# Attention scores as 32-row products of one head each, in place of block-diagonal products over all 128 rows

## What is computed

```python
x = x + xattn(layernorm(x), ctx, ctx, mask, Wq, Wk, Wv, Wo)
x = x + ffn(layernorm(x), wg, w1, w3, w2)
# xattn: 16 heads, head_dim 8
scores = einsum('bhqd,bhkd->bhqk', Q, K) / sqrt(8)
scores = where(mask == 0, -1e9, scores)
out    = einsum('bhqk,bhkd->bhqd', softmax(scores), V) ... @ Wo.T
# ffn: top 2 of 8 experts by x @ wg.T, each silu(x @ w1.T) * (x @ w3.T) @ w2.T
```

## Time and profile before

| | us |
|---|---|
| median of three executions | 288.39 |
| lowest and highest | 286.16, 289.48 |
| span of the profiled execution (first to last instruction) | 289.2 |
| TensorE busy, share of the span | 220.1 (76%) |
| VectorE busy | 214.5 (74%) |
| ScalarE busy | 131.9 (46%) |
| GpSimd busy | 109.8 (38%) |
| mean granted clock of TensorE | 0.877 of full speed |

### The profile page before, as it was taken

The page is one execution under the profiler, slowest core; times in us unless marked ns, Lnnn a source line. Parts: engine busy times, 40 slices in busy tenths (PEclk is TensorE's granted clock), DMA queues, the critical chain, the costliest instruction groups (busy, mean ns, idle before and its releaser), DMA issues.

```text
span 289.2 us, 5289 instructions
## 1 busy us (share of the span) xinstructions
PE 220.1 (76%) x1445; PEld 161.4 (56%) x1445; DVE 214.5 (74%) x619; ACT 131.9 (46%) x291; POOL 109.8 (38%) x120
## 2 busy tenths in 40 slices
PE   0787779998989988887667674688787789997620
PEld 0663456666757665665336542477566668886410
DVE  4779966688759867895977786568895568775596
ACT  5777127554665448342145546243334435453300
POOL 4310350121403070105486556104556565555530
PEclk9996579999999999979756799589899999999855
DMA  6954411353033302331602110421342232211807
GB/s 216 318 233 118 131 35 28 92 125 86 9 98 96 94 0 67 87 100 47 207 9 67 46 39 29 99 47 30 77 79 76 82 84 73 80 52 26 236 5 217
DMA packets 38108, 26.33 MB, mean 91 GB/s; under 512 B 4748, under 2 KB 35726, under 8 KB 37696
## 3 DMA queue, kind: packets, MB, share of 16 engines
q1 hardware_dynamic: 34848, 19.76, 25.5%
q0 software_dynamic: 2656, 5.40, 6.1%
q10 hardware_dynamic: 576, 0.83, 0.9%
HBM read 12.32 MB, written 6.31 MB: 64 GB/s over the span
## 4 chain that ended last, share of the span: by engine, by line
PE 42%; DVE 30%; issue 10%; SPq 8%; DMA 4%; ACT 2%; POOL 1%; another core or an unknown queue 1%; DVEq 0%; ACTq 0%; POOLq 0%
SPq L427 8%; PE bank L528 8%; DVE m_neg L1411 6%; PE bank L759 4%; PE bank L760 3%; PE bank L733 3%; PE bank L652 3%; DMA bd<-st 3%; PE bank L746 3%; PE bank L736 3%; PE bank L693 2%; PE bank L676 2%; PE bank L734 2%; PE bank L679 2%; PE bank L534 2%
## 5 line engine op out<-in xcount | busy, mean ns | idle before, releaser
L1411 DVE TENSOR_REDUCE m_neg<-bank 128x4 f32<-128x512 f32 x64 | 43.5, 684 | 15.4 <-PE bank L693 15.0
L1048 POOL DMA_INDIRECT ys<-big x39 | 38.1, 976 | 40.0 <-DVE big L1447 19.2
L923 ACT ACTIVATE big<-bank 128x512 f32<-128x512 f32 x64 | 37.4, 597 | 20.9 <-PE bank L679 20.0
L797 ACT ACTIVATE st<-bank 128x128 fp32r<-128x128 f32 (+1 forms) x78 | 22.6, 330 | 31.6 <-PE bank L746 16.1
L1004 POOL DMA_INDIRECT xg<-rows,rows_i x24 | 24.6, 1027 | 31.8 <-DVE rows_i L1218 11.6
L693 PE MATMUL bank<-bd,st 128*128 128x512 f32 x64 | 31.1, 509 | 4.7 <-DMA bd<-st 3.8
L676 PE MATMUL bank<-m_bd,ones_b 128*128 128x512 f32 x64 | 31.3, 489 | 2.1 <-ACT big L923 1.9
L759 PE MATMUL bank<-bd,st 128*128 x78 | 24.3, 332 | 9.8 <-DVE big L1447 6.2
L1355 DVE SCALAR_TENSOR_TENSOR st<-st_hi,cst,bank 128x512 fp32r<-128x512 f32 x32 | 23.3, 747 | 11.3 <-ACT st_hi L797 9.0
L1026 POOL TENSOR_TENSOR m_bd<-mT,cst 128x512 fp32r<-128x512 f32 x16 | 17.3, 1110 | 30.1 <-DVE mT L1334 30.0
L679 PE MATMUL bank<-bd,st 128*128 128x512 f32 x64 | 27.1, 423 | 0.0
(11 more groups left out here) (174 smaller groups left out, 514.0 us busy)
## 6 DMA issues: line engine op xcount, KB each, us to landing
bd<-st SPq DMA_DIRECT2D x126, 64.0 KB, 2.0
big<-xg SPq DMA_DIRECT2D x39, 64.5 KB
raw<-in_L_ffn_w SPq DMA_DIRECT2D x2, 1024.0 KB, 9.3
raw<-ys SPq DMA_DIRECT2D x6, 256.0 KB
x_all<-in_x SPq DMA_DIRECT2D x4, 256.0 KB, 4.5
rows<-in_mask_BxS_if POOLq DMA_DIRECT2D x4, 256.0 KB, 5.2
ctx_all<-in_L_ffn_w SPq DMA_DIRECT2D x1, 1024.0 KB
ctx_all<-in_ctx SPq DMA_DIRECT2D x3, 256.0 KB, 5.2
```

The costliest lines, as they stand in the source:

```text
L923: nc.scalar.activation(prob[n % 2][:, NJ * g:NJ * (g + 1), :].rearrange("p h q -> p (h q)"), s2[k % 2][:, :], ACT.Exp, scale=SCALE).then_i ...
L1048: pool.indirect_dma_start(ys, bass.IndirectOffsetOnAxis(xt[n % XR][:, D:RW].bitcast(I32), 0), y_sb[n % YR], None, bounds_check=PAIRS - 1, ...
L1411: nc.vector.tensor_reduce(m_neg[:, H * (b - 1) + NJ * g:H * (b - 1) + NJ * (g + 1)], s1[k % s1_ring(u)][:, :].rearrange("p (j q) -> p j q" ...
```

## The change

Neither block diagonals nor `m_bd` exist any more. A group of a tick is now "strip g of every stack": the four heads that stand in partitions 32g to 32g+31 of the four stacks. Each score is a product over these 32 rows alone, with `tile_position` naming the strip, 128 columns wide. The maxima come from a product of 32 rows of a constant selector `pick` with the same 32 rows of the transposed maxima `mT`. By-query scores of a tick use the strip `(g + 2) % 4`, so that they are on another strip than the by-key ones. The heads' order within values, maxima and the output weights follows suit (host side: `Wo` is laid out in another order), and `m_hl`, `mT` and the slices of the reductions and the exponentials are permuted with the same shapes and counts. ScalarE fills `pick` once (128x2048) after the first front instead of clearing six slots of the same size; the clearing of the second value buffer moves from VectorE to GpSimd. The load of the experts' third weights stays on SyncE's queue and has nothing ahead of it now.

```diff
-            def block_diagonal(k, n):
...
-                for j in range(2 if k and n == 0 else NJ):
-                    rows = slice(R * j, R * (j + 1))
-                    sp.dma_start(bd_slot(k, n)[rows, :, j, :].bitcast(F32), st[rows, u % 2, k, :, b * S:(b + 1) * S].bitcast(F32)
-                                 ).then_inc((kbd_ready if k else qbd_ready)[n % 3], 16)
...
+        def query_rows(g):
+
+            return (g + 2) % NJ
...
+            def scores(keys, queries, g):
+
+                if keys is not None:
+                    keys_wait(keys, g)
+                if queries is not None:
+                    queries_wait(queries, g)
+                for i in range(NG):
+                    if keys is not None:
+                        u, b = divmod(keys, QB)
+                        rows, tokens, o = slice(R * g, R * (g + 1)), slice(b * S, (b + 1) * S), s2[g % 2][:, i * P:(i + 1) * P]
+                        nc.tensor.matmul(o, pick[rows, NG * b + i, :], mT[rows, :], start=True, stop=False, tile_position=(R * g, 0))
+                    if queries is not None:
+                        v, c = divmod(queries, QB)
+                        own, mine = query_rows(g), slice(c * S, (c + 1) * S)
+                        part = slice(R * own, R * (own + 1))
+                        by_query = nc.tensor.matmul(s1[(NG * queries + g) % s1_ring(v)][:, i * P:(i + 1) * P], st[part, v % 2, 0, i, mine],
+                                                    st[part, v % 2, 1, i, mine], start=True, stop=True, tile_position=(R * own, 0))
+                    if keys is not None:
+                        by_key = nc.tensor.matmul(o, st[rows, u % 2, 1, i, tokens], st[rows, u % 2, 0, i, tokens],
+                                                  start=False, stop=True, tile_position=(R * g, 0))
...
-                            if b == 0:
-                                pe.wait_ge(mbd_ready, NG * (u - 1) + g + 1)
-                            nc.tensor.matmul(s2[k % 2][:, :], ones_b[:, b, :],
-                                             m_bd[:, NJ * g:NJ * (g + 1), :].rearrange("p h q -> p (h q)"),
-                                             start=True, stop=False)
-                            nc.tensor.matmul(s2[k % 2][:, :], st[:, (u - 1) % 2, 1, g, b * S:(b + 1) * S],
-                                             bd_slot(0, n)[:, g, :, :].rearrange("p j q -> p (j q)"),
-                                             start=False, stop=True).then_inc(s2_full, 1)
...
-                            nc.tensor.matmul(s1[k % s1_ring(u)][:, :], st[:, u % 2, 0, g, (b - 1) * S:b * S],
-                                             bd_slot(1, n)[:, g, :, :].rearrange("p j q -> p (j q)"),
-                                             start=True, stop=True).then_inc(s1_full, 1)
...
+                        scores(QB * (u - 1) + b if u >= 1 and b < QB else None, QB * u + b - 1 if u < NQ and b >= 1 else None, g)
...
-                nc.scalar.activation(bd[:, k, :], cst[:, C_ID:C_ID + 1].to_broadcast([P, NG * NJ * P]), ACT.Copy, scale=0.0
-                                     ).then_inc(bd_cleared, 1)
...
+                    copy(pick[:, :, :], cst[:, C_PICK:C_PICK + QB * NG].unsqueeze(2).to_broadcast([P, QB * NG, P])).then_inc(pick_ready, 1)
...
-                    for g in range(NG):
-                        nc.gpsimd.tensor_tensor(m_bd[:, NJ * g:NJ * (g + 1), :], mT[:, :].unsqueeze(1).to_broadcast([P, NJ, P]),
-                                                cst[:, C_HEAD + NJ * g:C_HEAD + NJ * (g + 1)].unsqueeze(2).to_broadcast([P, NJ, P]),
-                                                ALU.mult).then_inc(mbd_ready, 1)
```

More of the change, by code:

```diff
@@ L656, in values @@
-                last.then_inc(o_full, 1)
+                        for g in range(NG):
+                            h = NJ * g + 2 * half + i
+                            last = nc.tensor.matmul(ob[n % 2][R * g:R * (g + 1), half * P:(half + 1) * P],
+                                                    va[(n // QB) % 2][:, (n % QB) * H + h, :], prob[n % 2][:, h, :],
+                                                    start=(i == 0), stop=(i == 1), tile_position=(0, R * g))
+                last.then_inc(o_full, 1)
@@ L1325, in _ @@
             split_tokens(0)
-            ones_b_columns()
             for u in range(NQ + 1):
```

176 lines of the change are left out of this document (60 added, 116 removed).

## The result

The changed kernel takes 359.13 us (median of four executions, 355.93 to 361.44) against 288.94 us before: ratio 1.245, 95% interval 1.233 to 1.257; the ratio leaves out executions more than 1.5% above the fastest of their kernel. The span of the profiled execution is 358.5 us, 69.3 us more than before. That execution took 360.33 us, so 1.8 us lie around the span, and not the fraction of a microsecond that I had assumed. The sign was as forecast; the size was not, 359 us lies outside the range of 282 to 340.

What follows compares the result with a forecast made beforehand. TensorE was taken to bound stages 1 and 2: +4 each there, stage 3 +3, stage 4 +4.5, stage 0 -1.5, together +14 on the 289.2 us span: 303.2, or 302 us on the median; range 282 to 340.

Steps and rivals of the forecast that it cites:

- What bounds the kernel: TensorE fills the batches of stages 1 and 2 by itself; SyncE's queue of block diagonals runs beside it.
- the forecast's 0.4 us: Gain in each of stages 1 and 2, at the first query tick, from removing the block diagonals' DMAs on SyncE's queue.
- Strips of rows overlap: In a mixed tick the four query products run beside the eight key products: 0.88 us, against 1.32 without overlap.
- rival 1: Score ticks: strips of rows don't overlap, a mixed tick takes 0.44 us more, +28 in all, 316 us; chance 0.19.
- The price of 0.11 us: Score ticks: each 128-column product with its load costs 0.11 us on a strip, bounds 0.06 and 0.22.
- rival 4: Stages 1 to 4: granted clock falls to half because 32 rows work where 128 did; mixed tick 1.75 us; chance 0.04.
- rival 2: Score ticks: narrow fp32r products run at the fp32 rate, 0.22 us each on a strip; +69, 357 us; chance 0.15.
- Loads of 32 rows: Score products: a load's time goes by columns, so 32 rows take as long as 128; 0.11 us stands, 0.06 falls.
- Changes of mode: TensorE switching between strips and whole array: 0.15 us each, seven in place of two a batch, 0.75 us more.
- Stage 0: First reduction near 22.9 us, 1.9 us sooner, as a DMA wait and VectorE's clearing go: -1.5 us, other end 0.
- These are nothing: Stage 0: the clearing moved to GpSimd, busy 3.12 of 15.30 us, hides there; it was among items priced at nothing.
- Rival 3: Stages 0 to 4: strip loads cheap beside each other, mixed tick some 0.4 us, TensorE leaves the path: 279 us; chance 0.18.

Runs made afterwards that it cites:

- number 9: The kernel before without the 126 DMAs of the block diagonals and the waits for them (they stay zero): 286.14 us, ratio 0.988.
- number 1: The changed kernel with every score product over all 128 rows in place of 32, same count, columns and order: 319.15 us, ratio 1.103.
- number 7: The kernel before with by-query scores as four products of 32 rows and 128 columns on one strip, keys still block-diagonal: 305.22 us, ratio 1.055.
- number 5: The changed kernel with the eight key products of a tick over all 128 rows, the four query products on a strip behind them: 382.41 us, ratio 1.329.
- number 4: The changed kernel with one more product of 512 columns over 128 rows ahead of each tick, its result overwritten: 430.58 us, ratio 1.487.
- number 10: The changed kernel with GpSimd's clearing of the second value buffer held back until the first four score products are done: 355.07 us, ratio 1.230.
- number 8: The changed kernel with two ticks issued together, so that keys and queries use all four strips at once: 326.11 us, ratio 1.131.
- number 3: The changed kernel with every score product over 64 rows, keys and queries on opposite halves of the array: 358.45 us, ratio 1.243.
- number 11: The kernel before with the selector's maxima from four products of 128 columns over all rows, replacing `m_bd` and one of 512: 291.66 us, ratio 1.010.

## Why the prediction was wrong in its size

**What bounds the kernel: right.** TensorE filled stages 1 and 2 before and fills them after. The queue that led the chain was worth the forecast's 0.4 us in each of these stages, as number 9 shows.

**Strips of rows overlap: right.** A query product starts within hundredths of a key product; rival 1 fell. Where nothing overlaps (number 1), the run came to 319 us, next to rival 1's 316; that closeness is partly luck, since number 1 has fewer changes of mode than rival 1's sum and half clock in stage 4.

**The price of 0.11 us: right for full clock, wrong for this kernel.** This is the step that failed: "I take 0.11 us", "it enters all 768 products". I took both the price and its bounds of 0.06 and 0.22 at the clock of the rows they came from, and the clock of stages 1 and 2 from the earlier trace rows. Rows 9 held the price at half clock, and rival 4 used it, but with a chance of 0.04 and the argument "It is 1.00 in stages 1 and 2 now with TensorE just as full". That argument is what the runs refute. TensorE was just as full, 39.88 of 40.90 us, and got 0.50, so a product on a strip cost 0.21 us and not 0.11, a mixed tick 1.76 us against the forecast's 0.88, and from L613 to L613 in stage 2 it is 10.3 us (116.03 to 126.36) against 6.2. The Trainium skill, TensorE: Matmul & The Clock Gate, section What's actually happening, says that the gate is set by how busy the engine has been. Read as the share of time with a product under way, as I read it, this does not agree with the trace: 97% busy at half clock over 32 rows, 1.00 over 128 rows (number 1), and 96% busy at half clock in stage 4 of number 1.

**Rival 4's own sum held.** It took rival 2's working: +20 for stage 1, the same for stage 2, +14 for stage 3, +15 for stage 4, 357 us. Measured: +20.3, +19.7, +15.0, +13.0 and 359 us. The mixed tick of 1.75 us measured 1.76. Mechanism and sizes stood in the text; the weight was wrong. For stage 4 its reason, 32 rows where 128 worked, is only a part: with all 128 rows (number 1) the stage was at half clock too, and from its start to the end of the kernel it was 8.3 us more than before.

**Rival 2, narrow fp32r products at the fp32 rate: wrong,** though its time was right. Its price at full clock is 0.11 (0.11 in number 1, 0.11 at 49.80 us in the changed kernel). Without the clock column, the spacing of 0.21 us alone would have been taken for it; the time of 357 could not tell rivals 2 and 4 apart.

**Loads of 32 rows: right.** 0.11 us from load to load over 32 rows and 0.11 over 128 (number 1), and each load of 128 columns is shown 0.19 us long in both, at full clock. The Trainium skill, TensorE: Matmul & The Clock Gate, section LDWEIGHTS (loading the stationary operand), says that a load's time goes by its columns and not its rows. The trace agrees.

**Changes of mode: right in size.** 0.10 to 0.15 us at full clock (number 7), 0.14 to 0.20 at half clock (number 5), and 0.13 and 0.31 there around one product of 512 columns (number 4); the forecast had 0.15 for each.

**Stage 0: wrong in sign, -1.5 against +1.3.** The scores' part was right: the first reduction comes at 23.05 once the clearing is out of the way (number 10). The step that failed is "These are nothing", on the clearing that goes to GpSimd. I placed it in stage 0, where GpSimd is idle. GpSimd's order puts it at 10.24 us, beside VectorE's normalisation, which then took 2 us longer and held the whole front. The Trainium skill, GPSIMD Engine Reference, section Key points, says that GpSimd shares its SBUF interfaces with VectorE and that there is contention with VectorE's instructions in a 2-port perf mode or with two SBUF inputs. The trace shows contention, 4.07 against 2.08 us; it does not show which of these forms the operations have.

**Rival 3, faster: not in this order of the products.** Number 8 shows its mechanism (24 products in 1.0 us) and why it did not come: it needs four strips at once, and then TensorE waits for banks and the clock falls in between.

**What stays open.** Which property of the work the clock follows. The rows matter at equal width and order (number 1 in stages 1 and 2), the full products matter at equal strip work, by their width or by what goes with it (number 7 against 5), two halves side by side are not enough (number 3), four strips are sometimes (number 8). The level from which a stage starts may matter too: the same key products over all rows run at 1.00 in stages 1 and 2 of number 1 and at 0.50 in its stage 4. No run here isolates it, and none shows where a border lies. The forecast's own case, 32-row products at full clock, is seen only for the 3.2 us at the start of stage 1, since nothing that I tried held the clock up without changing the products; its sum of 302 us stays untested.

## What to carry to other kernels

When a change makes TensorE's products use fewer rows, price the ticks at both levels of the clock, even where the engine is never idle, and give the lower level real weight: here it doubled the price of the score ticks, and the zero-padded products over all rows were far cheaper (0.69 us for a mixed tick) than their exact 32-row parts (1.76). Do not take all rows as a warrant of the full clock either: with narrow products it was not won back once it was lost (number 1, stage 4). Read the granted clock of a stage first after such a change; the spacing of products alone cannot tell a slower clock from a dearer product. A small operation moved to GpSimd needs its place in time looked up, not only its engine's idle share, since VectorE beside it may pay.

## What the runs showed of the hardware that I had not expected

- TensorE busy 97% of 40.90 us on 32-row products: granted clock 0.50. The same products over 128 rows: 1.00 in stages 1 and 2 (number 1).
- The key products of 128 columns over all 128 rows, with TensorE busy 35.36 of 37.00 us, in a stage that began at half clock: 0.50 throughout (number 1, stage 4).
- Eight full products of 128 columns and four strip products in a tick: 0.50; two full products of 512 columns and the same four strip products: 1.00 (numbers 5 and 7).
- Strips of rows run side by side, start to start within 0.01 us, and on four strips 24 products pass in 1.0 us at full clock (number 8).
- A stationary operand that is one column spread to 128 loads at the usual price: four such products in 0.40 us (number 11).
- A clearing of 128x2048 on GpSimd held up VectorE's fp32 operations with scalars for about its whole length, 4.07 against 2.08 us; GpSimd's product of 128x512 beside the same operations (at 8.35 us here, 8.18 before) did not.
